# Routing of batch 0 pulled into attention 1, the shared experts of chunk 1 put behind the blocks, gathered rows weighed ahead of the shared sum

## What is computed

```python
x = layernorm(x + attention1(x))                    # 16 heads of 16, causal, (2, 1024, 256)
# expert layer, 8 experts, the best 2 of each token
scores = softmax(x @ gate_w.T)                      # (tokens, 8)
topk_w, topk_i = top_k(scores, 2)
topk_w = topk_w / sum(topk_w)
y = sum over the 2 chosen experts e of topk_w * ((silu(x @ wg[e]) * (x @ wu[e])) @ wd[e])
shared = (silu(x @ sg) * (x @ su)) @ sd             # inner width 256
x = layernorm(x + y + shared)
```

## Time and profile before

| what | value |
|---|---|
| median of 3 runs (lowest, highest) | 717.64 us (717.23, 723.69) |
| the profiled execution: its time, its span | 718.89 us, 717.1 us |
| mean granted TensorE clock, share of full speed | 0.931 |
| busy share of the span: PE, DVE, ACT, POOL | 90%, 58%, 55%, 32% |
| attention 1 on PE | 376.0 to 547.6 us |
| from there to the first block | 548.4 to 588.2 us |
| the blocks on PE | 588.2 to 672.4 us |
| from there to the end | 672.4 to 717.1 us |

### The profile page before, as it was taken

The page is one execution under the profiler, slowest core; times in us unless marked ns, Lnnn a source line. Parts: engine busy times, 40 slices in busy tenths (PEclk is TensorE's granted clock), DMA queues, the critical chain, the costliest instruction groups (busy, mean ns, idle before and its releaser), DMA issues. The chain is left out here.

```text
span 717.1 us, 11088 instructions
## 1 busy us (share of the span) xinstructions
PE 648.1 (90%) x3717; PEld 301.7 (42%) x3717; DVE 412.5 (58%) x1069; ACT 394.5 (55%) x565; POOL 233.0 (32%) x255
## 2 busy tenths in 40 slices
PE   4998899999998979999969999999999889999870
PEld 1654422222431344445422222243344657877450
DVE  1478616334466696979451333245738846547697
ACT  1235679988586832545438888867775133333100
POOL 0002533335412223113341344523122705325250
PEclk9998599999998989879898999999999999999996
DMA  8500143333224422310415545433570253575331
GB/s 276 168 0 16 43 74 54 58 57 57 39 37 68 67 71 70 67 53 1 67 32 86 83 79 84 81 64 62 90 225 1 97 190 126 175 235 164 102 119 59
DMA packets 52105, 62.68 MB, mean 87 GB/s; under 512 B 10150, under 2 KB 38819, under 8 KB 51891
## 3 DMA queue, kind: packets, MB, share of 16 engines
q1 hardware_dynamic: 48971, 53.50, 33.1%
q0 software_dynamic: 3072, 8.39, 3.8%
HBM read 28.79 MB, written 18.35 MB: 66 GB/s over the span
## 5 line engine op out<-in xcount | busy, mean ns | idle before, releaser
L1411 ACT ACTIVATE probs<-ps 128x1024 f32<-128x1024 f32 (+1 forms) x320 | 276.2, 963 | 67.6 <-PE ps L1329 67.5
L1329 PE MATMUL ps<-ops_mem 99*128 99x512 bf16 (+3 forms) x768 | 165.7, 338 | 10.8 <-issue 6.8
L1346 PE MATMUL ps<-probs,vstat 128*32 128x512 f32 (+3 forms) x1536 | 169.0, 512 | 7.1 <-DVE raw L1251 6.3
L1422 POOL TENSOR_SCALAR_AFFINE_SELECT probs<-probs 128x512 f32<-128x512 f32 x128 | 84.6, 661 | 210.6 <-ACT probs L1411 210.0
L1329 PEld LDWEIGHTS ps<-ops_mem 99*128 99x128 bf16 x768 | 58.3, 99 | 159.8 <-ACT probs L1411 86.3
L1251 DVE COPY raw<-ps 128x512 f32<-128x512 f32 x32 | 22.1, 691 | 141.9 <-PE ps L1346 141.7
L1346 PEld LDWEIGHTS ps<-probs,vstat 128*32 128x32 f32 x1536 | 31.3, 109 | 70.9 <-issue 47.6
L2278 PE MATMUL ps<-parts_mem 128*128 x184 | 47.4, 381 | 0.3 <-ACT parts_mem L2159 0.3
L2122 POOL DMA_INDIRECT yT<-made,w1qkv x32 | 30.5, 954 | 47.0 <-DMA made<-parts_mem 37.8
L2113 POOL DMA_INDIRECT sent<-xres,w1qkv x32 | 30.8, 964 | 39.8 <-DVE w1qkv L615 22.2
L1720 PE MATMUL ps<-ops_mem,w1qkv 128*128 128x512 f32 x64 | 36.4, 698 | 0.1
(11 more groups left out here) (214 smaller groups left out, 937.3 us busy)
## 6 DMA issues: line engine op xcount, KB each, us to landing
ops_mem<-parts_mem SPq DMA_DIRECT2D x276, 64.0 KB
sent<-in_zero_row SPq DMA_DIRECT2D x2, 2944.0 KB, 67.9
made<-parts_mem SPq DMA_DIRECT2D x46, 128.0 KB, 1.8
probs<-sent SPq DMA_DIRECT2D x4, 896.0 KB, 8.8
ops_mem<-parts_mem SPq DMA_DIRECT2D x66, 32.0 KB
yT<-in_xT SPq DMA_DIRECT2D x4, 512.0 KB, 7.6
xres<-in_x SPq DMA_DIRECT2D x1, 2048.0 KB, 14.5
parts_mem<-in_wgu SPq DMA_DIRECT2D x2, 1024.0 KB
```

The costliest lines, as they stand in the source:

```text
L1329: last = nc.tensor.matmul(ps[:, bank, o:o + CH - lo], kT[0:KDIM, buf, h if kh == GH else 0, kt * P:(kt + 1) * P], qT[0:KDIM, buf, h, c * C ...
L1346: last = nc.tensor.matmul(ps[32 * h:32 * h + 32, AV, lo:CH], vstat[:, i % 2, kt, h if kh == GH else 0, :], probs[:, s % PRING, h, 0:CH - l ...
L1411: nc.scalar.activation(o, banks, ACT.Exp, scale=score_scale).then_inc(s_exp, 1)
L1422: nc.gpsimd.affine_select(out=block_, in_=block_, compare_op=ALU.is_ge, fill=0.0, base=0, pattern=[[0, GH], [1, P]], channel_multiplier=-1 ...
```

## The change

The functions of the kernel keep their work; where they stand in each engine's program is changed.

1. `turn`, `logits` and their evictions for chunk 1 move from items 6 and 7 to item 6; `project(1, 1)` moves from step (5, 6) to (5, 4), and `turn(0, 0)` from (5, 11) to (5, 10). On DVE the scale and apply of chunk 1 stand `behind` item 5, and the evictions of both turns of chunk 0 stand after them.
2. Batch 0's `choose` moves from after `normalise(7, 0)` to ahead of `take(7, 0)`; its exponential moves on ACT from step (7, 8) to (7, 1); `rank` gets use 10 of bank 7 at step (7, 8), and `keep_rank` and `seat` stand ahead of `take(7, 1)` instead of in the tail. Three small weights of `rank` and `seat` are loaded ahead of the expert weights and get their own semaphore.
3. `gate_up(2)`, `gate_up(3)` and `down(1)` move on PE from ahead of the blocks to behind them, with ACT's silu and DVE's `multiplied` and `accumulate(1)`.
4. `weigh(0)` moves two turns of the loop earlier, `weigh(1)` into the loop (turns 43 and 44); for chunks 1 to 3 `weigh` starts from x, and the shared sum is added to it afterwards.

```diff
-            PROJECT, TURN, LOGIT = ((0, 1), (2, 3)), ((4, 5), (7, 8)), (6, 9)
+            PROJECT, TURN, LOGIT, RANKS = ((0, 1), (2, 3)), ((4, 5), (7, 8)), (6, 9), 10
...
-                for m, steps in enumerate((((4, 8), (4, 10)), ((5, 2), (5, 6)))):
+                for m, steps in enumerate((((4, 8), (4, 10)), ((5, 2), (5, 4)))):
...
-                for m, steps in enumerate((((5, 11), (6, 2)), ((6, 11), (7, 2)))):
+                for m, steps in enumerate((((5, 10), (6, 2)), ((6, 6), (6, 8)))):
...
-                if (i, s) in ((6, 4), (7, 4)):
-                    m = i - 6
+                if (i, s) in ((6, 4), (6, 10)):
+                    m = int(s == 10)
...
+                if (i, s) == (7, 8):
+                    pe.wait_ge(self.s_chosen, 1)
+                    pe.wait_ge(s_rank_w, 48)
+                    self.seven(pe, self.RANKS)
+                    self.rank(pe, 0, 7).then_inc(self.s_seven, 1)
...
                 if i == 5:
                     self.sum(dve, 1, 0)
+                    self.sum(dve, 1, 1)
                 if i == 6:
-                    self.of.k.then(self.of.statistics(0, y_sums[1]))
-                if i >= 6:
-                    self.evicted(dve, self.LOGIT[i - 6])
-                    self.keep_logits(i - 6, 7).then_inc(self.s_evicted, 1)
+                    self.keep_turned(dve, 0, 1)
+                    self.keep_seven(dve, 0)
+                if i == 7:
+                    self.choose(dve, 0)
...
                 if i == 5:
-                    self.sum(dve, 1, 1)
-                if i in (5, 6):
                     self.of.scale()
-                    self.of.apply(x_of(i - 5)).then_inc(self.s_norm, 1)
-                    self.keep_turned(dve, i - 5, 0)
+                    self.of.apply(x_of(0)).then_inc(self.s_norm, 1)
+                    self.norm(dve, 1)
+                    self.of.k.then(self.of.statistics(0, y_sums[1]))
+                if i == 6:
+                    self.keep_turned(dve, 1, 0)
+                    self.keep_turned(dve, 1, 1)
+                    self.keep_seven(dve, 1)
+                    self.shift(dve, 0)
                 if i == 7:
-                    self.shift(dve, 0)
-                    self.choose(dve, 0)
+                    self.evicted(dve, self.RANKS)
+                    self.keep_rank(7).then_inc(self.s_evicted, 1)
+                    dve.wait_ge(self.s_evicted, self.RANKS + 1)
+                    self.seat(dve, 0)
...
                 if i == 5:
-                    self.norm(dve, 1)
-                if i in (5, 6):
-                    self.keep_turned(dve, i - 5, 1)
+                    self.of.scale()
+                    self.of.apply(x_of(1)).then_inc(self.s_norm, 1)
+                    self.keep_turned(dve, 0, 0)
...
-                        if route and (i, s) == (NI - 1, 8):
+                        if route and (i, s) == (NI - 1, 1):
                             route.exp(act, 0)
...
                 logits(3)
-                gate_up(2)
-                gate_up(3)
-                down(1)
...
+                gate_up(2)
+                gate_up(3)
                 gate_up(4)
+                down(1)
                 gate_up(5)
...
-                route.keep_rank(dve, 0)
-                route.seat(dve, 0)
                 summed(2)
...
-                multiplied(2)
-                multiplied(3)
                 route.choose(dve, 1)
-                accumulate(1)
...
-                    if n == 38:
+                    if n == 36:
                         weigh(0, (0, 1))
+                    if n == 37:
+                        weigh(0, (2, 3))
                     if n == 39:
-                        weigh(0, (2, 3))
-                    if n == 41:
                         of = normalised(0, range(CT))
                         statistics(of)
+                    if n == 41:
+                        scaled(of, 0)
                     if n == 43:
-                        scaled(of, 0)
+                        weigh(1, (0, 1))
+                    if n == 44:
+                        weigh(1, (2, 3))
+                multiplied(2)
+                multiplied(3)
                 multiplied(4)
-                weigh(1, range(CT))
+                accumulate(1)
                 multiplied(5)
...
                 multiplied(6)
+                weigh(2)
                 accumulate(2)
-                weigh(2, range(CT))
...
+                weigh(3)
                 for n, (lo, hi) in enumerate(LAST):
...
-                    weigh(3, range(lo, hi))
```

88 lines of the change are left out of this document (44 added, 44 removed).

## The result

The change makes the kernel slower, by about as much as forecast: median 732.94 us (4 runs, 729.73 to 735.68) against 720.66 us before (4 runs), ratio **1.0186, 95% interval 1.0139 to 1.0233**. A ratio leaves out executions more than 1.5% above the fastest of their kernel and is worked out apart from the medians, so the two can differ by some tenths of a per cent. Timed once more in the last experiment it gave 1.0187 (1.0142 to 1.0233). The profiled execution after took 735.68 us, with a span of 733.9 us and a mean granted clock of 0.926. In the listings of order above, the rows of MATMUL, ISA and TENSOR_LOAD are PE's; only the rows behind the last of them are DVE's.

What follows compares the result with a forecast made beforehand. PE was taken to bound attention 1 and the blocks, DVE the stretch behind them. Waits, clock terms, the gain up to the blocks and the later losses summed to +14.1 us on 717.64, 731.7, placed at 730.5 (724 to 736).

Steps and rivals of the forecast that it cites:

- The wait at step 2 of item 6: Attention, second turn of chunk 0: PE waits for DVE's later eviction of the shared bank, +6.5 us (6.0 to 6.8).
- The clock behind it: Attention, behind the 6.5 us wait: PE runs at a lower clock after idling, +1.8 us (0 to 2.5).
- The wait for choose in item 7: Attention, item 7: PE waits for the take that choose now precedes on DVE, +2.2 us (1.4 to 2.5).
- The clock behind that: Attention, behind the wait for choose: lower PE clock, half of 1.8, +0.9 us (0 to 1.8).
- Turns and logits of chunk 1 in item 6: Attention: moved from item 7, the same PE work with DVE idle there; nothing, give or take 0.5 us.
- Attention as a whole: Attention 1, its waits and clock terms together: +11.4 us; 9 to 12 us longer was named as a sign.
- Up to the blocks: Tail before the blocks: first hidden transpose earlier without the moved experts, -9.4 us (-8.8 to -10.5), plus 0.9 for clock.
- The loop: Loop over blocks: weigh(1) added and turns at the lower clock, +1.6 us (0.9 to 2.4).
- Behind the loop: After the blocks: DVE waits for the moved gate_ups and down, +9.6 us (9.0 to 10.3).
- that attention takes the waits up: Rival, attention: ACT running ahead makes good PE's waits and clock, 720.3 us; at least half taken up, chance 0.12.
- That the tail overlaps: Rival, behind the loop: PE finishes gate_ups early, DVE bounds, -1.0 instead of +9.6 us; faster, chance 0.03.
- Cold PE everywhere: Rival, whole kernel: every clock term and parts 1, 2, 4, 5 at upper bounds, 736.9 us; above 737, chance 0.04.

Runs made afterwards that it cites:

- e11: The changed kernel itself, timed again beside e12 on the same chip; ratio 1.0187 to the kernel before, 733.40 us.
- e3: Changed kernel with gate_up(2), gate_up(3), down(1), their products and sum ahead of the blocks again, weighing as changed; ratio 1.0151, 734.28 us.
- e6: e5 with choose of batch 0 behind take(7, 0), rank two steps later on PE and seat behind take(7, 1); ratio 1.0044.
- e12: The kernel of e5 timed once more, beside e11 on the same chip; ratio 1.0033, 722.74 us.
- e1: Changed kernel with only the eviction of chunk 0's first turn back ahead of take(5, 1); ratio 1.0099, 729.74 us.
- e2: Changed kernel with the eviction of chunk 0's first turn behind normalise(5, 1) but ahead of chunk 1's scale and apply; ratio 1.0097, 732.25 us.
- e8: Kernel before, with ACT instead of DVE applying the norms of chunks 1, 2 and the first two pieces of chunk 3; ratio 0.9962, 717.99 us.
- e10: The kernel of e8 timed again on another chip, against the kernel before; ratio 0.995, median 718.91 us.
- e5: Changed kernel with both evictions of turned chunk 0 ahead of chunk 1's scale and apply on DVE; ratio 1.000.
- e7: e6 with the norms of chunks 1 and 2 behind the loop each ahead of a product on DVE; ratio 1.0021.

## Why the prediction was right, by its steps

The forecast of a slower kernel held, at 730.5 us (724 to 736) against 732.94. The sum of +14.1 us stands beside 1.86% of 720.66, +13.4 us. The base, 717.64 us, was 3.0 us under the median of before as it is now measured (720.66); as a difference the point forecast +12.9, against +12.3 by the medians. It was put 1.2 us under the full sum out of distrust of the clock terms. That this brought it nearer is luck, since the first of them turned out larger and not smaller. Term by term:

- **The wait at step 2 of item 6**, +6.5 (6.0 to 6.8): 6.41. The walk down DVE's program was right to 0.1 us.
- **The clock behind it**, +1.8 (0 to 2.5): **mis-sized, the largest error.** take(5, 1) to take(6, 0) is 8.22 us without the wait; less that and the wait, 5.35 us are left in the profiled execution, 2.35 in e11 and e3. The step priced one instruction after one idle; the lower level lasts over many. The term should have read 2.4 to 5.4.
- **The wait for choose in item 7**, +2.2 (1.4 to 2.5): 1.33. The step that failed is "so has its new place": I took the 4.67 us that choose had with GpSimd's masks beside it, but at the new place the masks are nearly absent (0.46 us) and it took 4.10. The Trainium skill's rule on contention (SBUF — State Buffer, Who interferes with whom) agrees with both windows; what was wrong was to apply it without looking at what GpSimd does there. With 4.10 the forecast would have been 1.6. Most of the rest is PE's side: it was ready for the product at 546.93 + 1.35 = 548.28, 7.2 us behind take(6, 1) at 541.08, and not at 6.5 to 6.8. That GpSimd's work is what makes choose longer stands on three lengths: 4.10, 4.67 and 6.34 us beside 0.46, 2.54 and 3.6 us of GpSimd (e6).
- **The clock behind that**, +0.9 (0 to 1.8): 1.57 in both executions of the changed kernel (21.26 and 21.27 us against 19.69 in e12, from take(6, 1) to take(7, 1), with the same wait in each), nothing in e1, e2, e3 and e12. Whether a wait of 1.33 us costs clock is thus not settled by its length; what else decides it stays open.
- **Turns and logits of chunk 1 in item 6**, 0: right. In e6, which has neither wait, take(6, 0) to take(6, 1) is 17.30 us (15.02 before) and take(6, 1) to take(7, 0) 6.06 (8.22 before): +2.3 and -2.2.
- **Attention as a whole**, +11.4: +14.6, and +11.75 in e11. The execution of before that I started from was itself slowed: take(6, 0) to take(6, 1) took 15.02 us in it and 13.46 in e8 and e10, which have the same attention. So its base was 1.6 us too long. The loss came without a wait: PE is busy throughout, its last idle time before was 0.24 us, and the clock is down. The window, of the kernel before:

```profile
512.70:516.30 3.60, 3.60 (x17) 0.61 (x14) 3.30 (x6) 3.14 (x4) 0.00 (x0) 0.53 0.64 105
```

- **Up to the blocks**, -9.4 with +0.9 for the clock, -8.5 net: -8.25. The mechanism is as forecast, the order of choose, hidden and transpose with it; the waits of PE were 1.01 and 0.47 us, not one of 2, and the clock took its share in the down of 6.71 us instead. Where that down was not slowed (3.70 us in e12) the stretch is 31.8 us, a gain of 11.6, outside the bound of 10.5: the bound left out that the same down took 5.39 us in the profile before.
- **The loop**, +1.6 (0.9 to 2.4): +1.96, and +1.8 in e12, but 2.9 in e11.
- **Behind the loop**, +9.6 (9.0 to 10.3): +8.4, in e11 and e12 too (51.18, 51.27), so this is no noise, and it lies outside the bounds. Small parts add up: the first gate_up ran at full clock (7.03 us for two, 3.5 each, where I took 3.96), the norm cost 6.16 - 0.6 = 5.6 us instead of 5.8, the last stretch gave 0.6 instead of 0.4, and the start in the profile before was taken 0.2 us late. The bound of 9.0 allowed for the first of these alone.

The rivals: that attention takes the waits up fell with the first table (+14.6). That the tail overlaps fell with the 14.2 us in which DVE waits. Cold PE everywhere, 736.9 us, was nearer than its small chance said: by its clock terms the profiled execution was that case in attention.

What the experiments add is where the loss lies. **Take the wait in item 6 away and the ratio falls from 1.0187 to 1.0033** (to 1.000 in e5), 11 to 13 us. Not all of this is the wait with the clock right behind it, for which the forecast gave 8.3. By the stretches, e11 against e12, that is 8.6 us (16.98 against 8.43); in the first execution of the changed kernel it is 11.8. The rest of the difference is the 1.6 us of clock in item 7 and 1.7 us up to the blocks, mostly a slower down, behind waits that e12 has too, and 1.1 us in the loop. No run shows that these follow from the wait in item 6: e3 has that wait and nothing of the kind in item 7, and e1 has 3.34 us of it and the same 31.79 us up to the blocks as e12.

The remaining terms, +5.8 in the forecast, are together worth 0 to 2.4 us by the ratios of e5 and e12. In e12's stretches they are +0.8: attention +2.1, up to the blocks -11.6, the loop +1.8, behind it +8.5. So the total came out right partly by luck: item 6 was put 0.3 to 3.5 us too low, the rest 3 us or more too high, most of that up to the blocks.

And it shows why the idea of the change gains nothing even without the wait: 9.4 us of PE work leave a stretch that PE bounds and arrive in one where DVE then waits for PE and ACT (e3). What would make the move pay is argued here and not run: DVE would need other work behind the loop to stand against these waits. weigh(1), 3.6 us, used to be that work and was moved away by the same change; no run puts it back behind the loop beside the moved experts. The nearest is e7, where the norms fill a part of the waits and 2.3 us come back.

## What to carry to other kernels

When an operation that evicts a shared bank is moved behind other work, list every later use of that bank: putting one eviction back moved the wait to the next use (e1), and only both together removed it (e5). Price an idle of TensorE by summing over everything behind it until the clock is back, not by one instruction. And work taken off one engine's stretch only pays if the engine is idle where the work goes and nothing on the way to the end waits for its result there. Last, when a short operation is to be moved beside another engine's work, read that engine's busy time in the very window it goes to: choose took 4.10, 4.67 or 6.34 us beside 0.46, 2.54 or 3.6 us of it.

## What the runs showed of the hardware

- After a wait of PE of 6.41 us the granted clock was 0.50 for 11.7 us in one execution, and for about 3 us in another, then 0.93. The wait is the same to the hundredth, the loss 5.35 and 2.35 us.
- A wait of 2.42 us was followed by the lower level too (0.51 over 3.2 us), and one of 1.33 us in two of six executions with it. The wait of 1.16 us ahead of the logits of chunk 2 is in every kernel; the down behind it took 3.70, 5.17, 5.39 and 6.71 us in e12, e11, before and after. It fell without any wait as well: 0.53 over 3.6 us of the kernel before, with PE idle for no more than 0.24 us at a time in the 8 us ahead. So the runs don't tell when the clock falls after a short wait, and a term for it can only be a range.
- The two levels give two durations for the same instruction: 1.95 and 3.58 us for 16 logits matmuls, 3.62 and 6.71 us for a down.
- DVE's operations can be held up by GpSimd's: a multiplication of 128x64 took 2.01 us instead of 0.22 under a GpSimd addition of 2.38 us, and ended 0.08 us after it (e6).
- ACT's apply of a norm to four tiles takes 2.08 us and DVE's 1.38 to 1.56; here ACT was idle, and with the slower engine the stretch behind the loop was 2.1 to 2.8 us shorter (e8, e10).
